# Second attention's output bias added by a 128-row matmul with the identity instead of a one-row matmul with ones

## What is computed

```python
xn = _layernorm(x, ln_gamma, ln_beta)
q = (xn @ w_q).reshape(B, SQ, NUM_HEADS, DIM_HEAD)
kv = context @ w_kv
...
scores = jnp.einsum('bqhd,bkhd->bhqk', q * SCALE, k)
attn = jax.nn.softmax(scores, axis=-1)
out = jnp.einsum('bhqk,bkhd->bqhd', attn, v).reshape(B, SQ, INNER)
out = out @ w_out + b_out
return out * jnp.tanh(gate[0])
```

## Time and profile before

| what | value |
|---|---|
| median of 3 executions | 1999.97 us |
| lowest and highest | 1995.61 and 2002.07 us |
| profiled execution, its own time | 2007.85 us |
| its span, first to last instruction | 2006.0 us |
| TensorE busy, share of the span | 1800.2 us, 90% |
| VectorE, ScalarE, GpSimd busy | 1418.5, 1132.0, 777.1 us |
| mean granted TensorE clock | 0.948 of full speed |

### The profile page before, as it was taken

One profiled execution on the slowest core, in us unless ns is written; L12 is line 12 of the kernel. 1 busy time (PEld: TensorE's weight loads), 2 busy tenths in 40 slices (PEclk: granted clock), 3 DMA queues, 4 the chain that ended last, 5 costly groups with the idle time before them and its releaser, 6 DMA issues.

```text
span 2006.0 us, 41321 instructions
## 1 busy us (share of the span) xinstructions
PE 1800.2 (90%) x15920; PEld 1491.4 (74%) x15920; DVE 1418.5 (71%) x2887; ACT 1132.0 (56%) x2812; POOL 777.1 (39%) x1160
## 2 busy tenths in 40 slices
PE   4798888899899899999999959999999999997646
PEld 3565656656899899999999847777777777876522
DVE  4567777763270489899888458999999999667421
ACT  1344555543334677777777447777777777744320
POOL 1212221101001143333332067788888787644100
PEclk8789999989999899999999979999999999998768
DMA  6444444322587576676676731222222221112599
GB/s 191 106 76 84 85 86 86 80 70 90 210 299 250 189 251 246 227 248 244 224 266 219 252 114 64 64 85 64 64 85 64 65 85 54 51 46 86 183 368 331
DMA packets 133974, 298.57 MB, mean 149 GB/s; under 512 B 13137, under 2 KB 77266, under 8 KB 118546
## 3 DMA queue, kind: packets, MB, share of 16 engines
q1 hardware_dynamic: 111378, 186.05, 29.9%
q0 software_dynamic: 18048, 105.69, 15.2%
q10 hardware_dynamic: 4352, 4.20, 0.6%
HBM read 207.80 MB, written 87.82 MB: 147 GB/s over the span
## 4 chain that ended last, share of the span: by engine, by line
PE 72%; DVE 13%; DMA 6%; issue 4%; POOL 3%; ACT 2%; SPq 0%; POOLq 0%; DVEq 0%
PE ps L1207 11%; PE ps L1193 11%; PE ps L1787 5%; PE ps L352 5%; PE ps L214 4%; PE ps L1818 4%; PE ps L1807 4%; PE ps L1773 4%; PE ps L358 3%; PE ps L454 3%; DMA R<-rp_scratch 2%; DVE NM L591 2%; PE ps L443 2%; PE ps L431 2%; DVE NM L180 2%
## 5 line engine op out<-in xcount | busy, mean ns | idle before, releaser
L191 ACT ACTIVATE P<-ps,NM 128x256 f32<-128x256 f32 x512 | 236.1, 473 | 164.5 <-DVE NM L180 164.4
L204 POOL TENSOR_TENSOR P<-P,RS 128x1024 f32<-128x1024 f32 x128 | 246.4, 1925 | 97.7 <-DVE RS L198 97.3
L591 DVE TENSOR_REDUCE NM<-ps 128x2 f32<-128x512 f32 x256 | 164.7, 686 | 115.4 <-PE ps L431 115.4
L1193 PE MATMUL ps<-XRP,W1P 128*128 128x256 f32 x1872 | 227.3, 281 | 2.8 <-DVE W1P L1277 2.8
L702 ACT ACTIVATE PT<-ps 128x512 f32<-128x512 f32 x256 | 138.7, 593 | 154.0 <-PE ps L443 151.6
L1193 PEld LDWEIGHTS ps<-XRP,W1P 128*128 128x128 f32 x1872 | 220.5, 190 | 3.4 <-DVE W1P L1277 3.4
L1207 PE MATMUL ps<-W2P,HP 128*128 128x256 f32 x1872 | 221.3, 277 | 0.0
L1207 PEld LDWEIGHTS ps<-W2P,HP 128*128 128x128 f32 x1872 | 217.7, 188 | 0.0
L138 POOL TENSOR_TENSOR LTMP<-RSTD 128x2 f32<-128x2 f32 (+1 forms) x156 | 32.4, 208 | 356.8 <-DVE RSTD L131 348.5
L180 DVE TENSOR_REDUCE NM<-ps 128x2 f32<-128x512 f32 x256 | 164.2, 683 | 1.1 <-PE ps L1773 0.5
L1241 ACT ACTIVATE HF<-ps,WE 128x256 f32<-128x256 f32 x312 | 129.1, 465 | 44.5 <-PE ps L1193 44.5
(11 more groups left out here) (220 smaller groups left out, 3859.5 us busy)
## 6 DMA issues: line engine op xcount, KB each, us to landing
k_scratch<-KVS SPq DMA_DIRECT2D x64, 256.0 KB, 3.2
KS<-k_scratch SPq DMA_DIRECT2D x64, 256.0 KB, 3.5
V<-v_scratch SPq DMA_DIRECT2D x16, 1024.0 KB, 6.6
rp_scratch<-RP SPq DMA_DIRECT2D x16, 1024.0 KB, 8.5
R<-rp_scratch SPq DMA_DIRECT2D x16, 1024.0 KB, 14.1
QS<-q_scratch SPq DMA_DIRECT2D x96, 128.0 KB, 4.5
v_scratch<-KVS SPq DMA_DIRECT2D x48, 256.0 KB, 2.3
ys_scratch<-YS SPq DMA_DIRECT2D x39, 256.0 KB, 8.2
```

Source lines behind the costliest of these rows:

```text
L191: i = e.activation(self.P[u % 4][:, c, :], PS[SB[n % 3]][:, y * 256:y * 256 + 256], ACT.Exp, bias=self.NM[:, u % 4, c:c + 1], accum_out=se ...
L204: e.tensor_tensor(p, p, self.RS[:, u % 4, :].unsqueeze(2).to_broadcast([128, 4, 256]), ALU.mult).then_inc(self.s_pn, 1)
L591: e.tensor_reduce(NM0[b % 2][:, :, 8 * h + p], PS[SB[(2 * u + h) % 3]][:, :].rearrange("p (l j) -> p l j", l=2), AX.X, ALU.max, negate=Tru ...
L1193: m = e.matmul(PS[p][:, hh * 256:hh * 256 + 256], W1P[i % 2][wi][:, cc * 1024 + hc * 128:cc * 1024 + hc * 128 + 128], XRP[i % 2][xi][:, cc ...
```

## The change

BO, the loaded bias, becomes 128 equal rows: its DMA reads the one row of 256 numbers and writes it to each of the 128 partitions. The gate's factor and the split in a high and a low half are worked out for 128 rows in place of one. ONER, a row of 128 ones, is replaced by EYE, the 128 by 128 identity, in a tile of the same size. The two matmuls of L1822 then have 128 rows: identity times 128 copies of the bias, which gives each token the bias again. The number and the order of instructions on every engine and in every queue stay as they are; only operands and their row counts differ.

```diff
-    ONER = mem("ONER", [128, 128], f32r)
+    EYE = mem("EYE", [128, 128], f32r)
...
-                    m = e.matmul(RB[:, 0:256], ONER[0:1, :], BOS[j][0:1, :], start=False, stop=(j == 1))
+                    m = e.matmul(RB[:, 0:256], EYE[:, :], BOS[j][:, :], start=False, stop=(j == 1))
...
-            e.tensor_copy(ONER[0:1, :], ones[0:1, :]).then_inc(s_bo, 1)
-            e.tensor_scalar(BO[0:1, :], BO[0:1, :], TG[0:1, 1:2], None, ALU.mult).then_inc(s_bo, 1)
+            e.tensor_copy(EYE[:, :], ident).then_inc(s_bo, 1)
+            e.tensor_scalar(BO[:, :], BO[:, :], TG[:, 1:2], None, ALU.mult).then_inc(s_bo, 1)
             w.wait_ge(s_bo, 2)
-            e.tensor_copy(BOS[0][0:1, :], BO[0:1, :]).then_inc(s_bo, 1)
+            e.tensor_copy(BOS[0][:, :], BO[:, :]).then_inc(s_bo, 1)
             w.wait_ge(s_bo, 3)
-            e.tensor_tensor(BOS[1][0:1, :], BO[0:1, :], BOS[0][0:1, :].bitcast(fp32), ALU.subtract).then_inc(s_bo, 1)
+            e.tensor_tensor(BOS[1][:, :], BO[:, :], BOS[0][:, :].bitcast(fp32), ALU.subtract).then_inc(s_bo, 1)
...
-        e.dma_start(BO[0:1, :], A["bo"]).then_inc(d_w0_w1, 16)
+        e.dma_start(BO[:, :], A["bo"].to_broadcast([128, 256])).then_inc(d_w0_w1, 16)
```

## The result

The changed kernel takes 1991.12 us in the median of 22 executions (1984.70 to 1999.38), the kernel before, run beside it, 2000.20 us in the median of 22 (1994.64 to 2009.63). The ratio is 0.9955, with a 95% interval of 0.9943 to 0.9968: 9 us, or 0.45%, faster, against the 10.1 us forecast.

A forecast was written before the change was run, and what follows sets the result against it. TensorE was taken to bound the attention: 31 pairs at 0.34 us gain 10.5, less 0.45 for the load, is -10.1 us, from the median of 1999.97 to 1989.9 us; range 1986.0 to 1996.0.

The forecast's parts named there:

- The bound: From first to last L1822, TensorE sets the pace: busy 545 of 557 us, while VectorE idles 52.3 us behind L1787.
- The price of a pair: The two L1822 bias matmuls cost TensorE 0.57 us before and 0.24 after, a gain of 0.34 us a pair.
- The number of pairs: Of the 32 bias pairs at L1822, 31 count: 31 x 0.34 = 10.5 us gained.
- The pair that was written off: Next to last half batch: its 0.34 us gain was to be lost in TensorE's 0.81 us wait for VectorE before L1787.
- The cause: At L1822, a change in row count between neighbouring matmuls loses time on entering and leaving; the change removes both.
- The path to XNP: From L1787 via VectorE and GpSimd to TensorE's wait for GpSimd's XNP: moves forward whole, wait unchanged (0.6 us at most).
- Rival A: At L1822, rows cost nothing and the 0.57 us ends an accumulation group; only load cost left, 2000.4 us; chance 0.10.
- B: One of a batch's two gains is absorbed in TensorE's waits for VectorE or GpSimd; 5.4 us left, 1995.0 us; chance 0.07.
- C: VectorE becomes the bound as L1877's and L150's work slows beside GpSimd; 10.5 us longer, 2010.5 us; chance 0.03.
- The load: Bias DMA in SyncE's queue ahead of the last expert store: 0.45 us later landing, nothing for issue; ends 0 and 1.65.
- The preparation on VectorE: VectorE's four bias-preparing instructions, now 128 rows high: no added time, upper end 0.4 us.
- The sum: Whole program: -10.5 + 0.45 = -10.1 us, forecast 1989.9 us, 0.5% faster; chance 0.80.

The follow-up runs named there:

- The load-only run: The changed kernel's bias load and preparation in 128 rows, but L1822 keeps one row, against the kernel before; ratio 1.0001 (0.9983 to 1.0018).

## Why the prediction was right

**The bound.** TensorE's pace was read rightly: shorter TensorE work showed one for one in the attention's length, as long as it stood outside TensorE's own waits, from 614.7 without a bias to 632.5 with one-row pairs.

**The price of a pair.** 0.57 before and 0.24 after were forecast; the chains show 0.58 and 0.23. It was essential to take starts, not durations: 47 ns a matmul in the durations stand against 0.17 in the starts.

**The number of pairs.** From the first to the last L1822 weight load it was 1238.4 to 1784.0 in place of 1247.9 to 1803.7, that is 10.2 us less, as 30 x 0.34 says. The pair that was written off fared better than forecast: the wait behind it grew from 0.81 to only 1.0 us, by 0.2 of the 0.34.

**The cause.** "I take the change of row count as the cause" went too far, without an effect on the sum. From 128 rows to 96, 97 or 120 the count changes and no gap comes. It is a change between classes, of which the runs show that 96 and more rows are one with 128, that 64 rows and fewer are outside it, and that 64 and one differ again. 96 rows would have brought the same gain. Nor is it rows alone: the prediction named a step between groups of equal row count without a gap, L1818 to L214, and overlooked one with a gap in every slot, from L214 to L1787. Both have 128 rows, but L1787's stationary tile is 64 columns wide:

```profile
1272.19 0.27 PE L214 MATMUL ps<-CST,P 128*128 128x128 f32 x1
1272.39 0.43 PE L1787 MATMUL ps<-PT,V 128*64 128x256 f32 x1
```

The start comes after 0.20 us, in place of L214's step of 0.11.

**What could take it back.** The path to XNP moved forward whole, and its wait stayed. VectorE's idle time fell by 13 us, more than the 10 forecast, without a new wait of TensorE's. Rival A, that rows cost nothing, is out. The Trainium skill, "TensorE: Matmul & The Clock Gate", Why this matters for your kernels, says that a matmul of 32 rows takes as long as one of 128. The page speaks of a single matmul. That is near right for durations in these traces (medians of 327 ns with 32 rows and 280 with 128), and doesn't hold for what a pair of 32 rows costs among full ones: 0.58 us in place of 0.23. Rivals B and C did not occur, though B's mechanism exists and was shown by the kernels with a bias in slot 5.

**The load.** 0.45 us were put down for a later landing of the last expert store, and nothing for its issue. The load-only run has an interval of some 3.6 us either way, so the whole time can't show either. The traces show the opposite split. Counted from the start of the last L1193, the store was issued after 12.35 us before and after 12.62 in the changed kernel, 0.27 later behind its queue; over all nine executions with the wide load it was 12.43 to 12.91. Yet it landed after 21.92 before and 21.67 after. The first score matmul comes 49.9 us after the same point before and 49.7 after; over all executions it is 49.6 to 50.3 with the wide load and 49.7 to 50.4 without. So no cost of the load is seen, and the half microsecond that was to appear ahead of the attention did not. The upper end for the issue of BO, 0.77 us, was too low: up to 1.16 came up. The preparation on VectorE, put at nothing, took as long as before: 0.35 us for the scaling in place of 0.33, and 1.87 for L1930 in both.

**The sum.** -10.1 forecast, -9.0 measured with an interval from -11.4 to -6.4. The attention's own -10.2, plus the last pair, makes -10.5, the forecast's own gain, and the load's +0.45 was not seen; the 1.5 us that are left to -9.0 lie within the interval, and no cause is claimed for it.

## What to carry over

Where TensorE is the bound, read its starts around every matmul that has fewer rows than its neighbours: a small one in a stream of full ones costs a gap on entering and one on leaving, of which the durations show about a quarter (47 ns a matmul of 0.17 us). Fill it up to the neighbours' height, or put it where the class changes anyway, or into a slot in which TensorE waits anyway; all three paid here, the second only by what the stretch shows. Once it has full height, its spare rows can carry a second term of the sum.

## What was not expected of the hardware

A matmul of 96 rows behaves as one of 128, while one of 64 costs among full ones what one of a single row does, though 64 rows and one are classes apart. A change of class costs on both sides, 0.09 us ahead of the new matmul and about 0.1 behind it, so a single odd matmul (0.46) is nearly as dear as a pair of them (0.58). The kernel has such changes elsewhere: in every slot, L1773's 64-row matmuls are followed by full ones, and the first start comes after 0.21 us. That a one-row pair turned into a 64-row one and set directly behind L1773 would cost no change of its own is a guess from this, and it wasn't tried.

The program's length scatters on both sides of this stage: the first score matmul started between 1158.3 and 1171.1 us over the fourteen profiled executions, and what followed the attention stretch took 196.8 to 207.5 us, while the attention stretches of the kernels with the same pairs agree within 1.6 us, and the inner ones within 0.2. For a change of 0.5% the stretch was the better measure.
